# The sum of the convolution's bias in slot 14 of its pass in place of slot 19

## The reference, cut to what matters

```python
x = x + 0.5 * ffn(layernorm(x))
x = x + attn(layernorm(x))          # the convolution block
x = x + 0.5 * ffn(layernorm(x))

def attn(x, ...):                   # long convolution through an FFT
    K = s4d_kernel(log_dt, log_A_real, A_imag, C_real, C_imag, L)
    y = irfft(rfft(x_t, 2 * L) * rfft(K, 2 * L), 2 * L)[:, :, :L]
    return gelu(y) @ W.T + b

def ffn(x, ...):
    h = silu(x @ w1.T * w1_s) * (x @ w2.T * w2_s)
    h = gelu(h @ h1.T * h1_s)
    h = gelu(h @ h2.T * h2_s)
    return h @ w3.T * w3_s
```

## Time and profile before

| what | value |
|---|---|
| median of 3 runs | 1303.97 us (1303.16 to 1304.44) |
| the profiled execution's own time | 1306.01 us |
| its span | 1304.2 us |
| TensorE busy | 1293.1 us, 99% |
| VectorE busy | 888.8 us, 68% |
| ScalarE busy | 762.9 us, 58% |
| GpSimd busy | 402.6 us, 31% |
| mean granted TensorE clock | 0.999 of full |

### The profile page before, as it was taken

The page is one execution under the profiler, slowest core; times in us unless marked ns, Lnnn a source line. Parts: engine busy times, 40 slices in busy tenths (PEclk is TensorE's granted clock), DMA queues, the critical chain, the costliest instruction groups (busy, mean ns, idle before and its releaser), DMA issues.

```text
span 1304.2 us, 17940 instructions
## 1 busy us (share of the span) xinstructions
PE 1293.1 (99%) x7039; PEld 653.2 (50%) x7039; DVE 888.8 (68%) x1768; ACT 762.9 (58%) x1245; POOL 402.6 (31%) x396
## 2 busy tenths in 40 slices
PE   9999999999999999999999999999999999999998
PEld 3454454644545445455454554545545455454544
DVE  5287768432546987988779887898877974454723
ACT  4664556845457467574775747757467564545433
POOL 6821377700012422633226333262332600001000
PEclk9999999999999999999999999999999999999999
DMA  8310000000010000000000000000000002221300
GB/s 314 136 41 9 9 1 17 1 9 9 1 53 13 2 15 1 17 1 1 17 1 17 9 9 17 17 12 14 9 17 17 9 17 74 81 81 56 138 1 19
DMA packets 45469, 41.80 MB, mean 32 GB/s; under 512 B 32704, under 2 KB 42432, under 8 KB 42688
## 3 DMA queue, kind: packets, MB, share of 16 engines
q1 hardware_dynamic: 45232, 40.56, 10.2%
q10 hardware_dynamic: 144, 0.02, 0.0%
HBM read 28.51 MB, written 4.19 MB: 25 GB/s over the span
## 4 chain that ended last, share of the span: by engine, by line
PE 93%; DVE 5%; issue 1%; ACT 1%; POOL 0%; POOLq 0%; DVEq 0%
PE psf L1421 66%; PE psf L1409 15%; PE psf L1433 7%; PE pss L1498 2%; DVE hab L645 1%; PE pss L1478 1%; DVE arena L602 1%; PE pss L1488 1%; PE pss L1449 1%; DVE xr L886 1%; DVE xr L674 0%; DVE psf L668 0%; DVE arena L605 0%; PE pss L1463 0%; DVE ht L657 0%
## 5 line engine op out<-in xcount | busy, mean ns | idle before, releaser
L1421 PE MATMUL psf<-hab,wall 128*128 128x512 f16 x4096 | 890.7, 379 | 2.8 <-DVE xr L674 1.8
L1421 PEld LDWEIGHTS psf<-hab,wall 128*128 128x128 f16 x4096 | 400.1, 98 | 482.4 <-DVE xr L674 3.2
L1180 ACT ACTIVATE psf<-psf,scf 128x512 f32<-128x512 f32 x256 | 168.7, 659 | 383.5 <-PE psf L1421 382.7
L645 DVE SCALAR_TENSOR_TENSOR hab<-psf,hab 128x512 f16<-128x512 f32 x256 | 174.9, 687 | 278.6 <-ACT hab L1173 277.7
L1409 PE MATMUL psf<-h,wall 128*128 128x512 f16 x1024 | 234.8, 381 | 1.0 <-ACT h L1184 0.7
L1173 ACT ACTIVATE hab<-psf 128x512 f16<-128x512 f32 x256 | 152.8, 597 | 8.1
L1409 PEld LDWEIGHTS psf<-h,wall 128*128 128x128 f16 x1024 | 99.8, 98 | 115.1 <-issue 2.5
L657 DVE SCALAR_TENSOR_TENSOR ht<-psf,scf,sil 128x512 f32<-128x512 f32 x128 | 93.9, 748 | 85.7 <-PE psf L1409 44.0
L1032 POOL TENSOR_SCALAR rs<-mv 128x4 f32<-128x4 f32 x16 | 5.3, 334 | 456.0 <-DVE mv L688 456.0
L1163 ACT ACTIVATE sil<-psf,scf 128x512 f32<-128x512 f32 x128 | 86.2, 685 | 83.0 <-PE psf L1409 82.2
L1433 PE MATMUL psf<-wall,hab 128*128 128x256 f16 x1024 | 117.1, 273 | 0.3
(11 more groups left out here) (143 smaller groups left out, 917.4 us busy)
## 6 DMA issues: line engine op xcount, KB each, us to landing
arena<-wh SPq DMA_DIRECT2D x8, 1024.0 KB, 5.4
g<-wh SPq DMA_DIRECT2D x6, 1024.0 KB, 9.2
out<-xr SPq DMA_DIRECT2D x15, 256.0 KB, 2.2
xr<-x SPq DMA_DIRECT2D x7, 512.0 KB, 5.0
arena<-w SPq DMA_DIRECT2D x3, 1024.0 KB, 5.1
g<-w SPq DMA_DIRECT2D x2, 1024.0 KB, 6.6
xr<-wh SPq DMA_DIRECT2D x2, 1024.0 KB, 9.5
g<-w SPq DMA_DIRECT2D x2, 512.0 KB, 6.0
```

What stands on the lines that cost most here:

```text
L645: e.scalar_tensor_tensor(out=hab[:, buffer(p), m, 1, :], in0=source(p), scalar=2.0 ** E2 if l else 1.0, in1=hab[:, buffer(p), m, 0, :], op ...
L1180: e.activation(bank, bank, ACT.Gelu, scale=scf[:, 2 + l, m:m + 1]).then_inc(s_gelu, 1)
L1421: ins = e.matmul(bank[:, :], WH[:, l, m // 2, k, ms], hab[:, buffer(p), k, part, :], start=(k == 0 and part == 0), stop=(k == KH - 1 and p ...
```

## The change

One constant: the slot in which `fixed` calls `bias_rows`.

```diff
 PROJECT_AT, RESIDUAL_AT = (0, 1, 2, 3), (1, 2, 3, 4)
-BIAS_AT = 19
+BIAS_AT = 14
 SUMS_AT, SCALES_AT = ((19, None), (3, 4)), 6
```

## The result

| what | before | after |
|---|---|---|
| median of 14 runs each | 1303.97 us (1303.16 to 1305.80) | 1307.34 us (1306.20 to 1310.13) |
| the profiled execution's own time | 1306.01 us | 1306.67 us |
| its span | 1304.2 us | 1304.9 us |
| TensorE busy | 1293.1 us | 1291.1 us |

The ratio is 1.0025, with a 95% interval from 1.0017 to 1.0034: the change makes the kernel slower by about 3.3 us. The 14 times of the changed kernel fall into two groups. Seven lie from 1306.20 to 1306.90 with a mean granted clock of 0.999 or 1.0, the other seven from 1307.78 to 1310.13 with 0.997 or 0.998, and the median lies between them.

What follows compares the result with a forecast made beforehand. The prediction took TensorE, busy 99% of the span, as the bound, so only its pauses count. New pauses of 5.8 us less 3.1 us of old ones gave +2.7 us on 1303.97, 1306.7 us, range 1304.5 to 1309.8.

Steps and rivals of the forecast that it cites:

- Where it bounds: TensorE, busy 99% of the span: only its pauses count; passes 6, 8 and 10 change, pass 12 costs nothing.
- The new pause: Before x_transform n=3 and the inverse in passes 6, 8 and 10: 1.89 to 1.90 us each, 5.8 us in all.
- The link: Late gate u0 delays ScalarE's split of u0, then x_out 0 and 1, whose banks x_transform n=3 and the inverse need.
- The old pauses: Waits in two blocks of 16 up products, passes 6, 8 and 10: 1.03 us a pass comes back, 3.1 us.
- The sum: Whole kernel: 5.8 - 3.1 = +2.7 us, ends +2.6 and +2.9, set on the median: 1306.7 us.
- the 0.2% line: Smallest difference a measurement can tell from no change, about 2.6 us; slower by more than that got 0.56.
- The profiled execution: The kernel before's profiled execution took 1306.01 us, 2.04 above the median, so the change was set on 1303.97.
- Only the loss: Rival: collisions with GpSimd persist and the old waits stay, so only +5.8 us, 1309.8; chance 0.08.
- the waits for L674: TensorE's waits for the row sums of d0 and d1 in passes 6, 8 and 10; 0.28 + 0.75 us, to vanish.
- Only the gain: Rival: gate u0's lateness does not reach x_out, so only -3.1 us, 1300.9; chance 0.04.
- Nothing visible: Rival: neither pause new nor old pause gone, or both of like size; 1303.4 to 1305; chance 0.12.
- The clock: Rival: granted clock falls after each new mid-pass pause, 3 x 1.7 us more, +7.8 us, 1311.8; chance 0.04.

Runs made afterwards that it cites:

- Cutting it: Changed kernel with the sum still in slot 14, x_out 0 and 1 moved from slot 17 to slot 16 of ScalarE's queue: 1300.48 us, ratio 0.9971.
- the kernel without the sum: Kernel before, its slot 19 sum cut to one token column of one feature: 1301.17 us, ratio 0.9981.
- The two later timings: The changed kernel timed again without edit beside the kernel before: 1306.65 us, ratio 1.0026, and 1306.84 us, ratio 1.0023.
- Half a sum: Against the kernel before, half of the tokens get the bias in slot 14 and half in slot 19: 1305.02 us, ratio 1.0001.
- both of these kernels: Against the kernel before: the sum in slot 15, 1313.73 us, ratio 1.0068; the sum twice in slot 14, 1318.18 us, ratio 1.0109.

## Why the prediction was right

- **Where it bounds.** That only pauses of TensorE count, and that three of four bias passes matter, held. Pass 12 kept its 22.20 us.
- **The new pause.** The link was as described: gate u0, split of u0, x_out 0 and 1, bank. Cutting it took the pause away. The size: I worked out 1.89 to 1.90 us plus 0 to 0.11, and took 0.04 for the last. The row after shows 0.11 us between the accumulator read and the sum, so the upper bound was right and my reason for the low value (that the sum uses all partitions, as the instructions with no gap do) was wrong: the gap is the same 0.11 us in front of the second x_low and in front of the sum. The nearest row, x_low behind such a read, had said 0.11. New pauses came to 3 x (0.97 + 1.03) = 6.0 us, not 5.8.
- **The old pauses.** 1.03 us a pass was right: 1.04 by the kernel without the sum. The prediction named both the sum and the longer split in front of d0's row sum, and the rows after say how they share it. The sum alone would not have made d0 late: 574.74 + 0.62 for a split of normal length gives 575.36, and d0 is ready at about 571.75 + 3.69 = 575.44. That is an estimate from the starts, as no run takes GpSimd's sum away. Counting from start to start was what gave it. The listed idle time of 0.59 us would have given 1.8 us for the three passes and a forecast of +4.
- **The sum.** +2.7 us with ends at +2.6 and +2.9; the stretches show +2.9 and the ratio 1.0025 is +3.3 us, with +2.2 to +4.4 as its interval. The median of 1307.34 lies inside the range; what it has above 1306.9 comes from how many of the 14 executions were of the longer group. The two later timings give 1306.65 - 1303.77 = 2.9 and 1306.84 - 1303.68 = 3.2 us. The three timings of the changed kernel gave 1.0025, 1.0026 and 1.0023, each above the 0.2% line in the middle and with a lower end below it.
- **The profiled execution.** I noted that it lay 2.04 us above the median and set the change on the median. The start was the reason, the clock above all (1.5 of 2.2 us), and a comparison of the spans would have read +0.7.
- **The rivals.** Only the loss, 1309.8: false, the waits for L674 went. Only the gain: false. Half a sum made gate u0 0.94 us late and passes 6, 8 and 10 cost 0.93 us, so nothing of it was absorbed; whether 0.1 us would be, as the rival has it, was not tried. Nothing visible: false, since both kinds of pause changed at nearly full size. The clock: false at 1.74 us in nine of nine profiled pauses, and true at 1.95 and 2.20 us, where it fell in four of six. The Trainium skill, "TensorE: Matmul & The Clock Gate", section "What's actually happening", which says that idleness brings the lower level back, is borne out by that. The seven longer of the 14 times, 1307.78 to 1310.13, have a mean clock of 0.997 or 0.998. A fall at the start explains 1.5 us and the kernel before has such executions too, but 1310.13 is 3.2 us above the longest of the other group. Whether the clock also fell behind a pause there stays open, as none of the seven was profiled.

## What to carry to other kernels

Moving 2 us of work on an engine that is a third idle can cost nearly its full length or nothing: what matters is the first instruction behind it on which the bounding engine hangs. From slot 14 to slot 16, from ahead of gate u0 to behind it, the same work was worth 6 us (1306.65 against 1300.70). Look for the idle gap that is long enough (here 2.48 us behind d1's row sum) and put it there. Judge a change of this size by start-to-start lengths of the stages it touches, since the span of one execution may differ by 2 us by what happens at its start.

## What the runs showed of the hardware

- **Behind short pauses the clock sometimes falls.** In a stream where TensorE is otherwise without a gap, pauses of 1.95 us were followed by the lower level in two of three cases of one execution, and pauses of 2.20 us, each 1.9 us of work behind a pause of 1.70, in two of three of another. Pauses of 1.74 us were followed by it in none of nine, in three executions. Over the 4 us behind the pause of pass 6 the granted clock was 0.57 in both of these kernels, and a fall cost 1.5 to 1.7 us. So few cases give no limit between 1.74 and 1.95 us.
- **Next to x_low there is a gap of 0.10 to 0.12 us.** It stands between the accumulator read of a split and x_low (560.36 to 560.47 before the change), between the two pieces of x_low (561.62 to 561.73), and now between x_low and a sum on 128 partitions (560.70 to 560.81). The sum behind a split in slot 19 had none (both at 572.53). x_low works on 64 partitions, and each piece reads one half of the partitions and writes the other. Which of the two makes the gap was not tried.
- **VectorE and GpSimd hold each other up.** The bias sum beside GpSimd's first sum made that one 3.80 us in place of 2.37, and the split behind it 2.84 in place of 0.69. The bias sum itself, which had started first, kept its 2.29 us. Apart, each has its own length. By the estimate above, the 2.15 us more of the split are what made d0's row sum late.
